# Quantised attention: the values' products of a pair stand behind the odd slot's projection, not ahead of it

## What is computed

```
def _fq(x, delta, zp, n_bits):
    xi = round(x / delta) + zp
    xq = clip(xi, 0.0, 2.0 ** n_bits - 1.0)
    return (xq - zp) * delta
def _attn(x, ctx, wq, wk, wv, wo, bo, dq, dk, dv, dw):
    q, k, v = heads(x @ wq), heads(ctx @ wk), heads(ctx @ wv)
    sim = einsum('bhid,bhjd->bhij', _fq(q, dq, 128.0, 8), _fq(k, dk, 128.0, 8)) * SCALE
    attn = softmax(sim, axis=-1)
    out = einsum('bhij,bhjd->bhid', _fq(attn, dw, 0.0, 8), _fq(v, dv, 128.0, 8))
    return merge(out) @ wo + bo
h1 = _ln(x, ln1_g, ln1_b)
x = _attn(h1, h1, a1_wq, ...) + x
h2 = _ln(x, ln2_g, ln2_b)
x = _attn(h2, context, a2_wq, ...) + x
```

## Time and profile before

| | |
|---|---|
| median of 3 runs | 2741.57 us (2741.06 to 2742.34) |
| profiled execution | 2741.51 us, span of the profile 2739.7 us |
| PE busy | 2575.7 us, 94% of the span |
| DVE, ACT, POOL busy | 1642.4 (60%), 1420.1 (52%), 678.6 us (25%) |
| the loop of 13 rounds | from about 127 to 907 us, 60.0 us a round |

### The profile page before, as it was taken

One profiled execution on the slowest core, in us unless ns is written; L12 is line 12 of the kernel. 1 busy time (PEld: TensorE's weight loads), 2 busy tenths in 40 slices (PEclk: granted clock), 3 DMA queues, 4 the chain that ended last, 5 costly groups with the idle time before them and its releaser, 6 DMA issues.

```text
span 2739.7 us, 54077 instructions
## 1 busy us (share of the span) xinstructions
PE 2575.7 (94%) x18304; PEld 2151.3 (79%) x18304; DVE 1642.4 (60%) x3945; ACT 1420.1 (52%) x3749; POOL 678.6 (25%) x1147
## 2 busy tenths in 40 slices
PE   5799999999999964999999999999999999999997
PEld 4566676676667642899999999999888888888885
DVE  6799999999999964634444443454443444444444
ACT  5688888888888862211112111123555555555554
POOL 1222222222222211323222222322221222222211
PEclk9899999999999977999999999999999999999998
DMA  4444444444444535311121211141111111111111
GB/s 151 94 95 100 93 98 97 100 92 96 99 93 96 93 63 144 105 69 69 54 84 54 77 56 74 61 150 66 47 54 38 54 54 46 46 46 54 46 38 39
DMA packets 335273, 211.06 MB, mean 77 GB/s; under 512 B 275568, under 2 KB 291952, under 8 KB 335216
## 3 DMA queue, kind: packets, MB, share of 16 engines
q1 hardware_dynamic: 335216, 210.34, 28.8%
HBM read 92.84 MB, written 50.33 MB: 52 GB/s over the span
## 4 chain that ended last, share of the span: by engine, by line
PE 56%; DVE 2%; issue 1%; ACT 1%; DMA 0%; POOL 0%; DVEq 0%; SPq 0%; POOLq 0%
PE AG L156 35%; PE Y L156 13%; PE XT L1314 3%; PE O L1337 2%; PE XT L1324 2%; PE XT L131 1%; DVE parts L1658 1%; DVE xhat L123 1%; PE Y L131 1%; PE O L1347 0%; DVE turned L185 0%; ACT stage L1554 0%; DMA stage<-in_ff_w_dram 0%; DVE mid_parts L1715 0%; POOL base L1870 0%
## 5 line engine op out<-in xcount | busy, mean ns | idle before, releaser
L156 PE MATMUL AG<-h_parts,up 128*128 128x256 f32 x6144 | 778.6, 284 | 13.4 <-DVE down L1639 10.1
L156 PEld LDWEIGHTS AG<-h_parts,up 128*128 128x128 f32 x6144 | 762.6, 192 | 26.0 <-issue 10.9
L599 ACT ACTIVATE e<-S,bias,qk_scale 128x256 f32<-128x256 f32 x1024 | 562.9, 569 | 113.5 <-POOL bias L805 113.5
L1522 ACT ACTIVATE gate<-AG,cols_pack 128x256 f32<-128x256 f32 x256 | 121.6, 475 | 668.8 <-PE AG L156 668.3
L1885 POOL TENSOR_TENSOR mid_parts<-mid_act,mid_parts 128x256 fp32r<-128x256 f32 x256 | 199.9, 781 | 1078.9 <-DVE mid_parts L1715 1078.9
L156 PE MATMUL Y<-down,mid_parts 128*128 128x512 f32 x1536 | 403.6, 399 | 0.0
L1708 DVE SCALAR_TENSOR_TENSOR mid_act<-AG,cols_pack,gate 128x256 f32<-128x256 f32 x256 | 123.4, 482 | 422.9 <-ACT gate L1522 421.9
L701 DVE TENSOR_REDUCE negmax<-S 128x4 f32<-128x1024 f32 x256 | 302.5, 1218 | 60.5 <-PE S L499 60.5
L156 PEld LDWEIGHTS Y<-down,mid_parts 128*128 128x128 f32 x1536 | 271.9, 189 | 68.7 <-issue 22.6
L719 DVE TENSOR_SCALAR pq<-e,rsum 128x256 uint16<-128x256 f32 x1024 | 292.1, 348 | 15.7 <-DMA pT<-pq 3.0
L147 PE MATMUL PJ<-w_a_wo,oT 128*128 128x512 f32 x512 | 239.4, 612 | 3.6 <-ACT oT L608 2.7
(11 more groups left out here) (125 smaller groups left out, 3411.4 us busy)
## 6 DMA issues: line engine op xcount, KB each, us to landing
stage<-in_ff_w_dram SPq DMA_DIRECT2D x48, 256.0 KB, 4.9
x_in<-in_x_dram SPq DMA_DIRECT2D x16, 512.0 KB, 3.9
ctx_in<-in_ctxT_dram SPq DMA_DIRECT2D x16, 512.0 KB, 3.6
mid_dram<-x SPq DMA_DIRECT2D x16, 512.0 KB, 2.7
own<-mid_dram SPq DMA_DIRECT2D x16, 512.0 KB, 3.3
own<-in_ctx_dram SPq DMA_DIRECT2D x16, 512.0 KB, 3.4
h_dram<-h3T SPq DMA_DIRECT2D x16, 512.0 KB, 2.6
k_dram<-own SPq DMA_DIRECT2D x16, 512.0 KB, 2.7
```

Of the source, the lines that this page charges most:

```text
L156: last = nc.tensor.matmul(acc, lhs(l), rhs(r), start=(start and i == 0), stop=(stop and i == 2))
L599: nc.scalar.activation(e[:, g % E_BUFS, i, :], S[g % 2][:, i // 2, i % 2, :], ACT.Exp, bias=bias[:, g % 2, i:i + 1], scale=qk_scale[:, ph. ...
L1522: nc.scalar.activation(gate[:, f % 2, :], AG[f % 2][:, TOK:2 * TOK], ACT.Gelu, bias=ff_b1[:, c:c + 1]).then_inc(gate_done, 1)
```

## The change

In an odd slot PE now does the projections ahead of the values' products. The turned fills stay ahead of both, and the output products stay behind the values' products. Nothing is added or removed, and every wait is carried along by its instruction.

```
                     for name, j in ph.steps(g):
                         if kind_of(name) in TURNED:
                             pe_fill(pe, at(ph.stage, ph.b, name, j))
+                    for name, j in ph.steps(g):
+                        if kind_of(name) not in TURNED and kind_of(name) not in ("o1", "o2"):
+                            pe_fill(pe, at(ph.stage, ph.b, name, j))
                     if g % 2:
                         if g >= 5:
                             pe_pv(pe, ph, g - 5)
                         elif prev:
                             pe_pv(pe, prev, g + GROUPS - 5)
                     for name, j in ph.steps(g):
-                        if kind_of(name) not in TURNED:
+                        if kind_of(name) in ("o1", "o2"):
                             pe_fill(pe, at(ph.stage, ph.b, name, j))
```

## The result

| | before | changed |
|---|---|---|
| median | 2741.88 us (4 runs, 2741.06 to 2742.34) | 2882.99 us (4 runs, 2877.27 to 2884.79) |
| profiled execution, its span | 2741.51, 2739.7 us | 2881.61, 2879.8 us |
| a round of the loop | 60.0 us | 69.5 us |

The changed kernel takes 1.0508 times as long, with a 95% interval of 1.0495 to 1.052: 141.1 us more, where 95.9 were forecast and 2856 us was the end of the range. The direction was right, and a third of the loss was missed.

What follows compares the result with a forecast made beforehand. PE was taken to bound the kernel by its own work, ACT close behind; 6.55 us a round times 14 is 91.7, plus 2.15 and 2 makes 95.9 onto 2741.57, about 2837 us, range 2816 to 2856.

Steps and rivals of the forecast that it cites:

- PE sets the pace and ACT is only just behind it: In a loop round PE is busy 57.62 of 60 us and sets the pace; scores wait for ACT's exponentials.
- hold of `oT`: In three slots a round, ACT's `oT` waits for the later values' products, 2.8 to 3.2 us idle in most.
- slot 3 of two: Slot 3 of phase two: late `oT` delays the exponentials, so the next scores start at 446.92 instead of 444.34, +2.58 us.
- Slot 7 of two: Slot 7 of phase two: late `oT` delays the first scores of phase one's slot 1, 460.13 instead of 458.74, +1.39 us.
- slot 1 of one: Slot 1 of phase one, a turned slot: values' products lose their cover there, between 0 and 0.33, taken as +0.05 us.
- The clock falls: Rival: PE's clock falls behind new waits, three times a round 1.5 to 3 us, some 2900 to 2960 us; chance 0.05.
- The late transpose: Slot 7 of phase one: late transpose delays DVE's `pq`, POOL's `x` and bias, so the exponentials; +0.82 us, bounds 0 and 1.7.
- the third rival: The transposes become the bound, by long landings or the `x2` store holding POOL: 1 to 2 us a round, 2850 to 2865; chance 0.07.
- The ends: Outside the loop: +2.15 us ahead of the last phase, and late transposes there and ahead of the loop, 2 us (0 to 5).
- ACT absorbs it: Rival: ACT's 10.7 us idle a round takes up the holds of `oT`, about 2742 us, no change; chance 0.04.
- +76 and +109: Range sums: a round at +5.3 us gives +76, one at +7.4 gives +109 with ends at 5.
- The signs to look for: Profile after: round about 66.5 us, `oT` idle 2.8 to 3.2 us, PE waiting ahead of three scores, clock 1.00 in the loop.

Runs made afterwards that it cites:

- The kernel without holds: Changed kernel with the values' products directly behind the scores again in slots 3 and 7 of phase two and slot 3 of phase one; 2773.1 us, 1.0108 of before.
- the kernel at 1.0007: Kernel before with only slot 7 of phase two changed and that half's `oT` moved to slot 1 of the next phase, behind the exponentials; 2745.41 us, 1.0007.

## Why the prediction was right, and where it failed

**PE sets the pace and ACT is only just behind it**: right. Each hold of `oT` came out at 3.0 us (2.8 to 3.2 forecast), and the three alone cost 5.84 us a round against 5.68. In slot 3 of two the 0.48 us from PV to `oT` of the earlier trace rows holds (493.20 to 493.68), and so does +2.58. In slot 7 it is 0.56 (440.21 to 440.77), part of why one 1 grew by 1.60 and not 1.39.

**Slot 7 of two, "+1.39", and slot 1 of one, "+0.05"**: this is the step that failed most. The first was near alone (+1.40, by luck, with the clock low in 1 of 14 rounds), the second was 0.14 us in one 3 and up to 0.5 with what followed it, and together they cost 3.76. The sum treated the slots as independent, "each slot as if all ahead of it had been on time", and put the cost of the clock at nothing. Together they put two waits around 1.1 us of transposes, and in every round some of what stands there, the product at least, ran at the low clock. 2.04 us × 14 = 29 us, two thirds of the miss of 44 in the span (140.1 against 95.9).

**The rival "The clock falls"** was the missing cause, with a chance of 0.05 that was too low. It named three places, each of the three waits ahead of S; it happened at one, the one with the longest wait and with light work and a second wait behind it; which of these singles it out was not tested apart. The argument against it rested on the earlier trace rows, one S that took 0.40 us behind a wait of 2.92. That S shows only the clock at the moment PE resumes. The trace of before shows what came behind that very S, in windows of PE over S and PV and over the wait that followed, and in the next S:

```profile
1014.78:1015.55 0.77, 0.73 (x16) 1.00 0.37 68
1015.65:1021.37 5.72, 0.00 (x0) 0.50 0.55 85
...
1021.37 0.61 PE L499 MATMUL S<-kT,qT 32*128 32x256 bf16 x8 [5.86 <-ACT e L599]
```

The clock was low within 1 us of the S that was taken as proof against it. Its price for one place, 1.5 to 3 us, was right on the mean (2.04; single rounds 1.3 to 2.7).
The Trainium skill, page "TensorE: Matmul & The Clock Gate", section "A second HAM failure mode: psum-queue depth-cycling", reports a kernel in which small idles between groups of matmuls came often enough to let the clock swing between its two levels. That agrees with the low clock behind waits of 0.62 and 0.71 us above. I had weighed only the section on long waits; the waits of its example are longer than any that PE has in this loop, so "by that rule this second rival would be the forecast" took it further than it goes.

**The late transpose, "+0.82"**: in the right place, too small. The step two 3 grew by 1.25. Against S of slot 1, `pq` came 1.52 us later than before (it started 1.44 us ahead of S, now 0.08 behind), where 1.27 was taken; and the store behind the transpose on SP, named in the third rival but left out of the term, held POOL's `x` by some 0.14 us more. The kernel without holds also has 0.52 us in four other steps of which the terms had 0.05. In the changed kernel the steps other than one 3 exceed the forecast by 0.82 together, 11 us in 14 rounds.

**The ends, "2.15 + 2"**: 7 us were measured (140.1 − 14 × 9.50), the upper bound of these terms. The first scores of the loop come 3.42 us late (121.94 before, 125.36 now), though the first scores of all came 2.02 us early (43.22, 41.20). In between the clock was 0.80 on average instead of 0.85, and one output product took 8.80 us instead of 7.11. How much of this the change made, by late transposes or by the clock, stays open.

**"ACT absorbs it"**: wrong for this order of ACT, as argued; it is right where `oT` stands behind the exponentials, as the kernel at 1.0007 shows.

**The range** took in the case of the transposes by half and the clock not at all. Its own sums, +76 and +109, give 2818 to 2851; the 2816 to 2856 stated is wider by up to 5 us without a reason. The signs to look for came true for the holds and failed for the clock (0.95 over the round, not 1.00). The clock's case at its one place and the other steps measured as here would have given 2837 + 29 + 11 = 2877 without the ends.

Open: what decides, beside the two waits of slot 1, whether the clock falls in a round, and why in every other round of two kernels. More buffers for `pq`, which would tell the transposes' part from the store's, weren't tried.

## What to carry to other kernels

Before an instruction moves later on the engine that sets the pace, look on the other engines for the in-order instruction that waits for it, and what stands behind that one: here a 0.33 us step moved by 3 us cost up to 2.6, and in slot 7 of two nothing once its reader stood behind the exponentials. Read SP as such an engine too: a store behind a late transpose is late with it. Where two new waits come close together around light matmuls, price the clock for the product behind them, look at the clock of some us behind the row that you take as proof, and add the slots up in one schedule rather than each by itself.

## What the runs showed of the hardware that was not expected

A wait of 2.22 us on PE with one of 0.38 behind it left the clock at 1.00 in 13 of 14 rounds of one kernel, and let it fall in 13 of 14 of another with more waits elsewhere. With one of 0.71 us behind 1.8 us of scores and transposes (481.90 to 483.71) the clock was low in every round, in some only from the product on (a mean of 0.63 over 484.42 to 489.00). Even 0.62 and 0.71 us were followed by a slow product in 5 of 14 rounds of one kernel, and 0.80 and 0.71 in none of another. The first matmuls behind a wait can run at full speed and the clock still be low within 1 us (1014.78 to 1015.65). And twelve matmuls of no use in each round, put into the wait, made the program 26 us faster.
